# Carries of a pair of steps computed together on POOL in a selective state-space scan

## The chip, the cores and the metric

The kernel runs on one core of one Trainium2 chip. What counts is the device time of one execution in microseconds (us), as the median of several runs. The core's engines are TensorE (PE; its weight loads are listed as PEld), VectorE (DVE), ScalarE (ACT), GpSimd (POOL) and SyncE (SP), which issues the DMAs.

## What is computed

The reference is one block with a conditioned normalisation, a selective state-space layer that is run forwards and backwards over the sequence, and a gated MLP. Its input is 16 sequences of 256 positions with 256 channels, in float32. The part that sets the time is the recurrence, which is run over 512 inner channels with 64 states each:

```python
def step(hst, ins):
    dt_t, B_t, C_t, x_t = ins
    dA = jnp.exp(dt_t[:, :, None] * A)
    hst = hst * dA + (dt_t * x_t)[:, :, None] * B_t[:, None, :]
    y_t = jnp.einsum('bds,bs->bd', hst, C_t)
    return (hst, y_t)
...
_, ys = jax.lax.scan(step, h0, (tm(dt), tm(Bm), tm(Cm), tm(xs)))
y = jnp.swapaxes(ys, 0, 1) + xs * Dskip
return y * jax.nn.silu(z) @ out_w
```

## The kernel before

The main phase makes 16 passes (8 pairs of sequences, two directions). The 128 partitions hold 2 sequences by 64 states. A pass cuts its 256 positions into 8 chunks of 32 (`TC`), and the 512 channels into 16 groups of 32. One **step** j is one chunk and one group of channels, so a pass has 128 steps (`JP`), 16 to a chunk, and is taken two steps at a time: pair i is the steps 2i and 2i+1, 64 pairs a pass. The engines run the same list of steps side by side and are held together by semaphores:

- **PE**, step j: eight small matmuls write the step's inputs into the PSUM buffer `u[j % 2]` (L968), four write the exponents of step j+2 (L979), and eight add up a part of the last half chunk's output (L998). Before it, it waits for `ud` of the pair (POOL, L501), for `dd` of the pair after it (POOL, L492) and for the scan j-2, which frees `u`.
- **ACT**, step j: `put_carry(j)` (L755) copies the carry `hin` into the first column of each of the 32 channels of `u[j % 2]`. Then comes `decay(j + 2)`: twice an exponential of the first column (`e0`, named b_first in the rows, L736) and one of the other 31 columns (`dA`, L737). Then one piece of side work.
- **DVE**, step j: one scan over 1024 columns (L829), after `put_carry(j)`.
- **POOL**, pair i: `turn_dt(i + 2)` (L492), the carry of step 2i, side work, `turn_u(i + 1)` (L501), at i%8 = 2 `spread_c` (L514) and at i%8 = 6 `first_inputs` (L520), the carry of step 2i+1, side work. `turn_dt(i + 2)` waits for scan 2i-3.

A carry is needed from the second chunk of a pass on, that is for the steps 16 to 127 of each pass. It is `hin = e0 * hs_last + u0`: the first decay of the chunk times the last state of the same channels in the chunk before (`carry_in`, a product at L527 and a sum at L532, both over 32 columns), plus the first input. `e0`, `hm` and `hin` have four buffers (`NM`), by j % 4. In `hs` the two steps of a pair stand in neighbouring words (the last axis, `kp`).

The **side work** prepares the next pass: projections, SiLU and softplus of its inputs. It is written as generators (`unit`), of which each engine takes one piece a step, in the passes 0 to 14. On POOL pieces start with pair 2. One SiLU of the eight takes four steps: a clamp (L432) after the even carry of one pair, and the product (L438) after the odd carry of the next. The product waits for ACT's third sigmoid piece (L605). The four softplus parts follow, each with four pieces in four steps in a row (L444, L447, L451, L456), at the steps 42 to 45, 54 to 57, 68 to 71 and 80 to 83. Every second pass (0, 2 to 12) has four more pieces of normalisation in a row at the steps 102 to 105 (L423). POOL takes all of this in the order in which it is written.

After the main phase an output phase of some 450 us multiplies by the output weights and runs the MLP. The change doesn't touch it.

Of the kernel before, what the change touches and what calls it, by code (L numbers as in the profile page):

```python
# [6 lines left out]
ALU = mybir.AluOpType  # L7
# [19 lines left out]
TC = 32  # L27
# [5 lines left out]
STEPS = RT // 2 * SPN  # L33
# [25 lines left out]
def main_phase(nc, x, cond, w_mod, b_mod, w_in, w_xp, dt_bias, a_log, mod, scr):  # L59
# [4 lines left out]
    with ctx:  # L64
        def sb(name, shape, dt=fp32):
            return ctx.enter_context(nc.sbuf_tensor(name, shape, dt))
# [81 lines left out]
        hm_made = sem("b_hm_made")  # L148
# [6 lines left out]
        e0_done = sem("b_e0_done")  # L155
        hin_made = sem("b_hin_made")
        carried = sem("b_carried")
        scanned = sem("b_scanned")
# [37 lines left out]
        CSTEPS = JP - STEPS  # L196
# [18 lines left out]
        def scanned_to(p, j):  # L215
            return p * JP + (j + 1 + SCAN0)
# [4 lines left out]
        def carried_to(p, j):  # L221
            return p * CSTEPS + (j - STEPS + 1 + CARRY0)
# [10 lines left out]
        def place(j):  # L233
            c, k = divmod(j, STEPS)
            return c, k, k % 2, k // 2
# [6 lines left out]
        with nc.Block() as block:  # L242
# [162 lines left out]
            def _(pool):  # L405
# [99 lines left out]
                def spread_c(p, c):  # L505
                    n = c % 2
                    g = p * NCH + c
                    pool.wait_ge(c_loaded[n], loaded_to(p, c, C_DMAS))
                    if g >= 2:
                        pool.wait_ge(summed, QT * (2 * g - 2))  # L510
                    for b in range(CB):
                        first = b * QG
                        last = first + (QG - 1) * (QR + 1) + 1
                        nc.gpsimd.tensor_tensor(cw[:, n, :, first:last:QR + 1], cr[:, n, :, :],  # L514
                                                hmask[:, b:b + 1].unsqueeze(2).broadcast_to((P, QT, QG)), ALU.mult).then_inc(cw_made, 1)

                def first_inputs(p, c):
                    pool.wait_ge(f_loaded[c % 2], loaded_to(p, c, F_DMAS))
                    flat = u0[:, c % 2, :, :, :].rearrange("p k v d -> p (k v d)")
                    nc.gpsimd.tensor_tensor(flat, flat, b0[:, c % 2, :].broadcast_to((P, DI)), ALU.mult).then_inc(u0_made, 1)  # L520
                    pool.wait_ge(u0_made, p * (NCH - 1) + c)

                def carry_in(p, j):
                    c, k, kp, v = place(j)
                    pool.wait_ge(e0_done, p * (2 * CSTEPS) + 2 * (j - STEPS + 1))
                    pool.wait_ge(scanned, scanned_to(p, j - STEPS))
                    nc.gpsimd.tensor_tensor(hm[:, j % NM, :, :].rearrange("p h d -> p (h d)"),  # L527
                                            e0[:, j % NM, :, :].rearrange("p h d -> p (h d)"),
                                            hs[:, v, :, TC - 1, kp], ALU.mult).then_inc(hm_made, 1)
                    pool.wait_ge(hm_made, p * CSTEPS + (j - STEPS + 1))  # L530
                    pool.wait_ge(carried, carried_to(p, j - NM))
                    nc.gpsimd.tensor_tensor(hin[:, j % NM, :, :], hm[:, j % NM, :, :],  # L532
                                            u0[:, c % 2, 2 * kp:2 * kp + 2, v, :], ALU.add).then_inc(hin_made, 1)

                def ahead(p, i, turn, last):
                    if i < PAIRS:
                        turn(p, i)
                    elif not last:
                        turn(p + 1, i - PAIRS)

                def one_pass(p, last, side):
                    for i in range(PAIRS):
                        c, v = divmod(i, STEPS // 2)
                        ahead(p, i + 2, turn_dt, last)
                        if c:
                            carry_in(p, 2 * i)
                        if i >= 2:
                            next(side, None)
                        ahead(p, i + 1, turn_u, last)
                        if v == 2:  # L550
                            spread_c(p, c)
                        if v == STEPS // 2 - 2 and c + 1 < NCH:
                            first_inputs(p, c + 1)
                        if c:
                            carry_in(p, 2 * i + 1)
                        if i >= 2:
                            next(side, None)

# [3 lines left out]
                for p in range(PASSES):  # L562
                    one_pass(p, p == PASSES - 1, unit(p + 1) if p + 1 < PASSES else wait_steps(0))
# [894 lines left out]
```

## Time and profile before

| | |
|---|---|
| median of 3 runs | 5534.01 us (5531.95 to 5535.1) |
| time of the profiled execution | 5537.5 us |
| its span | 5535.8 us |
| mean granted TensorE clock of the span | 0.985 |
| main phase with carries, first to last `hin` | 155.1 to 5074.8 us |
| busy, PE / DVE / ACT / POOL | 5360.0 / 4737.6 / 3368.7 / 3918.4 us |

All three runs lie within 3.2 us of each other. A busy PE is not one at its peak: the ends of its matmuls are modelled, and they overlap. For the other engines a gap between two instructions is time in which the engine stood still, and the profile names what ended it. In the timelines an entry can stand for several instructions that follow each other without a gap (x2, x3). Every pass with side work looks like every other to within a few tenths of a microsecond, so pass 5 (it starts about 1674 us into the span) stands for them here. In pass 5 scan 16 starts at 1713.43 us, scan 42 at 1782.36 us and scan 80 at 1880.9 us. Pass 6 is 313.9 us later.

### The profile page before, as it was taken

To read this page: it belongs to the slowest core of one execution; us is meant where nothing else is said; L and a number is where in the kernel's file an instruction comes from. 1 tells how busy PE (TensorE), PEld (TensorE's weight loads), DVE (VectorE), ACT (ScalarE), POOL (GpSimd) and SP (SyncE) were. 2 spreads that over 40 slices of the span, in tenths; PEclk is the share of its full clock that TensorE was granted. 3 is DMA by queue.
4 is the path that set the end of the run, shared out by engine and by line. 5 is a ranking of instruction groups with operands and counts; after the bars stand their busy time and mean duration, and the time that the engine had idled before them with its cause. 6 is when DMAs were issued, how large, how long until landed. Compare 5 with 4: busy or idle time off the path is not lost. (4 is left out here: it accounts for less than half of the span.)

```text
span 5535.8 us, 127746 instructions
## 1 busy us (share of the span) xinstructions
PE 5360.0 (97%) x43632; PEld 2426.9 (44%) x43632; DVE 4737.6 (86%) x2419; ACT 3368.7 (61%) x11178; POOL 3918.4 (71%) x6629
## 2 busy tenths in 40 slices
PE   5999999999999999999999999999999999997898
PEld 3444444444444444444444444444444444443444
DVE  2898998989898998989898999989898998997433
ACT  4666666666666666666666666666666666564111
POOL 4777777787877777787877778787877778674221
PEclk8999999999999999999999999999999999998999
DMA  3111112111111112111111112111111111112552
GB/s 100 55 46 53 52 36 64 36 60 35 56 47 53 51 34 63 38 53 44 55 46 53 51 35 64 37 54 44 55 46 49 52 35 47 31 28 81 157 156 64
DMA packets 433131, 306.57 MB, mean 55 GB/s; under 512 B 215920, under 2 KB 336240, under 8 KB 432496
## 3 DMA queue, kind: packets, MB, share of 16 engines
q1 hardware_dynamic: 428272, 294.39, 17.8%
q8 instruction: 340, 5.57, 0.4%
q10 hardware_dynamic: 4224, 4.19, 0.2%
q14 instruction: 295, 2.42, 0.1%
HBM read 187.27 MB, written 111.15 MB: 54 GB/s over the span
## 5 line engine op out<-in xcount | busy, mean ns | idle before, releaser
L829 DVE TENSOR_TENSOR_SCAN b_hs<-b_dA,b_u 128x1024 f32<-128x1024 f32 x2048 | 4552.4, 2271 | 425.4 <-ACT b_u L755 351.8
L979 PE MATMUL b_ex<-b_dd,b_aw 32*128 32x512 f32 x8192 | 3081.6, 643 | 23.0 <-POOL b_dd L492 15.0
L737 ACT ACTIVATE b_dA<-b_ex 128x496 f32<-128x496 f32 x4096 | 2286.3, 588 | 254.2 <-PE b_ex L979 234.5
L968 PE MATMUL b_u<-b_ud,b_bw 32*128 32x256 f32 x16384 | 2344.8, 403 | 36.3 <-DVE b_hs L829 33.8
L968 PEld LDWEIGHTS b_u<-b_ud,b_bw 32*128 32x128 f32 x16384 | 1385.9, 184 | 1135.6 <-issue 697.8
L492 POOL TENSOR_TENSOR b_dd<-b_dr,b_mask 128x512 f32<-128x512 f32 x1024 | 1073.2, 1048 | 646.2 <-DVE b_hs L829 629.9
L998 PE MATMUL b_y<-b_hs,b_cw 128*32 128x256 f32 x16384 | 1261.3, 390 | 2.7 <-DVE b_hs L829 2.7
L755 ACT ACTIVATE b_u<-b_hin 128x32 f32<-128x32 f32 x1792 | 361.2, 202 | 1438.8 <-PE b_u L968 1040.8
L979 PEld LDWEIGHTS b_ex<-b_dd,b_aw 32*128 32x128 f32 x8192 | 1057.2, 183 | 161.3 <-ACT b_dA L737 104.0
L501 POOL TENSOR_TENSOR b_ud<-b_ur,b_mask 128x512 f32<-128x512 f32 x1024 | 1082.4, 1057 | 0.1
L998 PEld LDWEIGHTS b_y<-b_hs,b_cw 128*32 128x32 f32 x16384 | 348.6, 108 | 1196.7 <-issue 1150.2
L736 ACT ACTIVATE b_first<-b_ex 128x16 f32<-128x16 f32 x3584 | 629.7, 176 | 27.5 <-PE b_ex L979 22.9
L527 POOL TENSOR_TENSOR b_hm<-b_first,b_hs 128x32 f32<-128x32 f32 x1792 | 480.2, 268 | 120.6 <-ACT b_first L736 108.6
L532 POOL TENSOR_TENSOR b_hin<-b_hm,b_u 128x32 f32<-128x32 f32 x1792 | 450.5, 251 | 140.4
L1132 POOL TENSOR_TENSOR c_gs<-c_gs,c_sz 128x512 f32<-128x512 f32 x64 | 78.9, 1271 | 300.4 <-DVE c_gs L1338 300.4
L874 PE MATMUL b_job<-b_hT,b_win 128*128 128x512 f32 x488 | 276.0, 648 | 0.0
L887 PE MATMUL b_job<-b_xs,b_wxp 128*128 128x512 f32 x488 | 273.7, 644 | 0.0
L438 POOL TENSOR_TENSOR b_xs<-b_xs,b_cl 128x512 f32<-128x512 f32 x64 | 82.1, 1283 | 113.3 <-ACT b_cl L605 113.3
L432 POOL TENSOR_SCALAR b_cl<-b_xs 128x512 f32<-128x512 f32 x64 | 95.0, 1485 | 88.6 <-ACT b_xs L615 88.3
L748 ACT ACTIVATE b_ysb<-b_y 128x128 f32<-128x128 f32 x512 | 120.5, 308 | 8.9 <-PE b_y L998 8.9
L874 PEld LDWEIGHTS b_job<-b_hT,b_win 128*128 128x128 f32 x488 | 73.5, 189 | 118.6 <-issue 88.8
L444 POOL TENSOR_TENSOR b_nd<-b_wy,b_ey 128x512 f32<-128x512 f32 x64 | 82.0, 1281 | 56.5 <-ACT b_wy L638 56.5
(128 smaller groups left out, 2492.6 us busy)
## 6 DMA issues: line engine op xcount, KB each, us to landing
b_u<-scratch_ut SPq DMA_DIRECT2D x256, 128.0 KB, 2.9
scratch_y<-b_ysb SPq DMA_DIRECT2D x128, 256.0 KB, 2.3
scratch_xs<-b_xs SPq DMA_DIRECT2D x64, 256.0 KB, 2.2
scratch_sz<-b_sd SPq DMA_DIRECT2D x64, 256.0 KB, 3.3
scratch_dt<-b_sd SPq DMA_DIRECT2D x64, 256.0 KB, 2.0
scratch_ut<-b_uT SPq DMA_DIRECT2D x64, 256.0 KB, 2.3
b_ur<-scratch_ut SPq DMA_DIRECT2D x1024, 16.0 KB
b_dr<-scratch_dt SPq DMA_DIRECT2D x1024, 16.0 KB, 1.7
```

The lines of the kernel that those rows point to most:

```text
L492: nc.gpsimd.tensor_tensor(dd[:, i % NPR, :, :], dr[:, c % 2, v:v + 1, :].broadcast_to((P, TT, TC)), mask[:, :].unsqueeze(2).broadcast_to(( ...
L501: nc.gpsimd.tensor_tensor(ud[:, i % NPR, :, :, :], ur[:, c % 2, :, v * TT:(v + 1) * TT].unsqueeze(3).broadcast_to(shape), mask[:, :].unsqu ...
L527: nc.gpsimd.tensor_tensor(hm[:, j % NM, :, :].rearrange("p h d -> p (h d)"), e0[:, j % NM, :, :].rearrange("p h d -> p (h d)"), hs[:, v, : ...
L532: nc.gpsimd.tensor_tensor(hin[:, j % NM, :, :], hm[:, j % NM, :, :], u0[:, c % 2, 2 * kp:2 * kp + 2, v, :], ALU.add).then_inc(hin_made, 1)
L736: nc.scalar.activation(e0[:, j % NM, h, :], src[:, :, 0], ACT.Exp).then_inc(e0_done, 1)
L737: nc.scalar.activation(dA[:, j % NDA, h, :, 1:TC], src[:, :, 1:TC], ACT.Exp).then_inc(exp_done, 1)
L755: nc.scalar.activation(u[:, j % 2, :, 0:H:TC], hin[:, j % NM, :, :], ACT.Copy).then_inc(carried, 1)
L829: nc.vector.tensor_tensor_scan(hs[:, v, :, :, kp].rearrange("p d t -> p (d t)"), dA[:, j % NDA, :, :, :].rearrange("p h d t -> p (h d t)") ...
L874: ins = nc.tensor.matmul(job_bank(n)[:, :], win[:, k, i * P:(i + 1) * P], hT[:, q % DIRS, k, :], start=(k == 0), stop=(k == MB - 1))
L968: ins = nc.tensor.matmul(dst[:, :, tb, :], bw[row(r), c % 2, tb, :], ud[row(r), j // 2 % NPR, tb, :, :], start=(tb == 0), stop=(tb == NTB ...
L979: nc.tensor.matmul(e[bank_of(2 * j + h)][:, :], aw[row(r), p % DIRS, v, :, :].rearrange("p b s -> p (b s)"), dd[row(r), j // 2 % NPR, :, : ...
L998: ins = nc.tensor.matmul(y[q * QR:(q + 1) * QR, cols], cw[:, n, q, g * QR:(g + 1) * QR], hs[:, f * (SPN // 2):(f + 1) * (SPN // 2), :, q * ...
```

## The change

`carry_in` is called once a pair, for the even step 2i, and makes both carries: one product and one sum over 64 columns where there were two of each over 32. The call after `turn_u`, for step 2i+1, is gone. The waits are those that the odd step had: for its `e0` (ACT's `decay(2i+1)`), and for `put_carry(2i-3)`. The semaphores `hm_made` and `hin_made` go up by two.

```diff
                 def carry_in(p, j):
+
                     c, k, kp, v = place(j)
-                    pool.wait_ge(e0_done, p * (2 * CSTEPS) + 2 * (j - STEPS + 1))
-                    pool.wait_ge(scanned, scanned_to(p, j - STEPS))
-                    nc.gpsimd.tensor_tensor(hm[:, j % NM, :, :].rearrange("p h d -> p (h d)"),
-                                            e0[:, j % NM, :, :].rearrange("p h d -> p (h d)"),
-                                            hs[:, v, :, TC - 1, kp], ALU.mult).then_inc(hm_made, 1)
-                    pool.wait_ge(hm_made, p * CSTEPS + (j - STEPS + 1))
-                    pool.wait_ge(carried, carried_to(p, j - NM))
-                    nc.gpsimd.tensor_tensor(hin[:, j % NM, :, :], hm[:, j % NM, :, :],
-                                            u0[:, c % 2, 2 * kp:2 * kp + 2, v, :], ALU.add).then_inc(hin_made, 1)
+                    two = slice(j % NM, j % NM + 2)
+                    pool.wait_ge(e0_done, p * (2 * CSTEPS) + 2 * (j + 1 - STEPS + 1))
+                    pool.wait_ge(scanned, scanned_to(p, j + 1 - STEPS))
+                    nc.gpsimd.tensor_tensor(hm[:, two, :, :].rearrange("p j h d -> p j (h d)"),
+                                            e0[:, two, :, :].rearrange("p j h d -> p j (h d)"),
+                                            hs[:, v, :, TC - 1, :].rearrange("p d k -> p k d"), ALU.mult).then_inc(hm_made, 2)
+                    pool.wait_ge(hm_made, p * CSTEPS + (j + 1 - STEPS + 1))
+                    pool.wait_ge(carried, carried_to(p, j + 1 - NM))
+                    nc.gpsimd.tensor_tensor(hin[:, two, :, :].rearrange("p j h d -> p (j h) d"),
+                                            hm[:, two, :, :].rearrange("p j h d -> p (j h) d"),
+                                            u0[:, c % 2, :, v, :], ALU.add).then_inc(hin_made, 2)
...
                         if v == STEPS // 2 - 2 and c + 1 < NCH:
                             first_inputs(p, c + 1)
-                        if c:
-                            carry_in(p, 2 * i + 1)
                         if i >= 2:
                             next(side, None)
```

POOL's queue in the SiLU stretch of a pass, from one product of the side work to the next two steps on; b_first is `e0`, b_e0_done tells that ACT has made it. Before:

```order
L438 TENSOR_TENSOR b_xs<-b_xs,b_cl 128x512 [waits b_chain]
L492 TENSOR_TENSOR b_dd<-b_dr,b_mask 128x512 [waits b_scanned]
L527 TENSOR_TENSOR b_hm<-b_first,b_hs 128x32 [waits b_scanned,b_e0_done]
L532 TENSOR_TENSOR b_hin<-b_hm,b_u 128x32 [waits b_carried,b_hm_made]
L432 TENSOR_SCALAR b_cl<-b_sd 128x512 [waits b_silu_made,b_freed]
L501 TENSOR_TENSOR b_ud<-b_ur,b_mask 128x512 [waits b_scanned]
L527 TENSOR_TENSOR b_hm<-b_first,b_hs 128x32 [waits b_scanned,b_e0_done]
L532 TENSOR_TENSOR b_hin<-b_hm,b_u 128x32 [waits b_carried,b_hm_made]
L492 TENSOR_TENSOR b_dd<-b_dr,b_mask 128x512 [waits b_scanned]
```

The same place with the change:

```order
L438 TENSOR_TENSOR b_xs<-b_xs,b_cl 128x512 [waits b_chain]
L492 TENSOR_TENSOR b_dd<-b_dr,b_mask 128x512 [waits b_scanned]
L529 TENSOR_TENSOR b_hm<-b_first,b_hs 128x64 [waits b_scanned,b_e0_done]
L534 TENSOR_TENSOR b_hin<-b_hm,b_u 128x64 [waits b_carried,b_hm_made]
L432 TENSOR_SCALAR b_cl<-b_sd 128x512 [waits b_silu_made,b_freed]
L501 TENSOR_TENSOR b_ud<-b_ur,b_mask 128x512 [waits b_scanned]
L492 TENSOR_TENSOR b_dd<-b_dr,b_mask 128x512 [waits b_scanned]
```

The odd step's product and sum, which stood behind the clamp and `ud`, now stand ahead of both, in the same instructions as the even step's.

POOL's queue at the first softplus part (steps 42 to 46), before:

```order
L444 TENSOR_TENSOR b_nd<-b_wy,b_ey 128x512 [waits b_logged]
L501 TENSOR_TENSOR b_ud<-b_ur,b_mask 128x512 [waits b_scanned]
L527 TENSOR_TENSOR b_hm<-b_first,b_hs 128x32 [waits b_scanned,b_e0_done]
L532 TENSOR_TENSOR b_hin<-b_hm,b_u 128x32 [waits b_carried,b_hm_made]
L447 TENSOR_TENSOR b_nd<-b_ln,b_nd 128x512 [waits b_nd_made]
L492 TENSOR_TENSOR b_dd<-b_dr,b_mask 128x512 [waits b_scanned,b_d_loaded1]
L527 TENSOR_TENSOR b_hm<-b_first,b_hs 128x32 [waits b_scanned,b_e0_done]
L532 TENSOR_TENSOR b_hin<-b_hm,b_u 128x32 [waits b_carried,b_hm_made]
L451 TENSOR_TENSOR b_sd<-b_pre,b_nd 128x512 [waits b_sz_stored0,b_nd_made]
```

And with the change:

```order
L444 TENSOR_TENSOR b_nd<-b_wy,b_ey 128x512 [waits b_logged]
L501 TENSOR_TENSOR b_ud<-b_ur,b_mask 128x512 [waits b_scanned]
L447 TENSOR_TENSOR b_nd<-b_ln,b_nd 128x512 [waits b_nd_made]
L492 TENSOR_TENSOR b_dd<-b_dr,b_mask 128x512 [waits b_scanned,b_d_loaded1]
L529 TENSOR_TENSOR b_hm<-b_first,b_hs 128x64 [waits b_scanned,b_e0_done]
L534 TENSOR_TENSOR b_hin<-b_hm,b_u 128x64 [waits b_carried,b_hm_made]
L451 TENSOR_TENSOR b_sd<-b_pre,b_nd 128x512 [waits b_sz_stored0,b_nd_made]
```

Each softplus piece now waits behind a product that needs the `e0` of the pair's odd step; the small instructions between `ud` and the next piece are gone. On ACT, DVE, PE and SP the instructions and their order are unchanged.

## Rows read from the trace of the kernel before

**Rows 1.** Page, costliest groups: line, engine, out<-in, shape, count | busy us, mean ns | idle before, releaser

```profile
L829 DVE TENSOR_TENSOR_SCAN b_hs<-b_dA,b_u 128x1024 f32<-128x1024 f32 x2048 | 4552.4, 2271 | 425.4 <-ACT b_u L755 351.8
...
L501 POOL TENSOR_TENSOR b_ud<-b_ur,b_mask 128x512 f32<-128x512 f32 x1024 | 1082.4, 1057 | 0.1
...
L527 POOL TENSOR_TENSOR b_hm<-b_first,b_hs 128x32 f32<-128x32 f32 x1792 | 480.2, 268 | 120.6 <-ACT b_first L736 108.6
L532 POOL TENSOR_TENSOR b_hin<-b_hm,b_u 128x32 f32<-128x32 f32 x1792 | 450.5, 251 | 140.4
```

**Rows 2.** Waits, whole span: engine, line, who ended them, us in total, times, longest

```profile
ACT b_u L755 <- PE b_u L968: 1040.8, 1290, 2.1
...
ACT b_u L755 <- POOL b_hin L532: 397.3, 373, 2.6
DVE b_hs L829 <- ACT b_u L755: 351.8, 602, 2.3
```

**Rows 3.** DVE's timeline, pass 5, scans 10 to 15: start, length, [idle before <-releaser]

```profile
1698.51 6.64 DVE L829 TENSOR_TENSOR_SCAN b_hs<-b_dA,b_u 128x1024 f32<-128x1024 f32 x3 [0.20 <-PE b_u L968]
1705.82 2.29 DVE L829 TENSOR_TENSOR_SCAN b_hs<-b_dA,b_u 128x1024 f32<-128x1024 f32 x1 [0.67 <-PE b_u L968]
1708.53 4.46 DVE L829 TENSOR_TENSOR_SCAN b_hs<-b_dA,b_u 128x1024 f32<-128x1024 f32 x2 [0.42 <-PE b_u L968]
```

**Rows 4.** DVE's timeline, pass 5, the quiet scans 96 to 101

```profile
1914.80 13.15 DVE L829 TENSOR_TENSOR_SCAN b_hs<-b_dA,b_u 128x1024 f32<-128x1024 f32 x6
```

**Rows 5.** DVE's scans alone by stretch: from:to, length, busy (count), PEclk, DMA, GB/s

```profile
1712.00:1760.90 48.90, 41.61 (x19) 1.00 0.15 46
2025.80:2074.70 48.90, 41.70 (x19) 1.00 0.15 46
1782.30:1799.60 17.30, 13.61 (x6) 1.00 0.19 54
...
1880.90:1894.20 13.30, 13.12 (x7) 1.00 0.24 72
```

**Rows 6.** POOL's timeline, pass 5, SiLU stretch, around the carries of step 20

```profile
1733.34 0.27 POOL L527 TENSOR_TENSOR b_hm<-b_first,b_hs 128x32 f32<-128x32 f32 x1
1733.69 0.25 POOL L532 TENSOR_TENSOR b_hin<-b_hm,b_u 128x32 f32<-128x32 f32 x1
1733.90 1.48 POOL L432 TENSOR_SCALAR b_cl<-b_sd 128x512 f32<-128x512 f32 x1
...
1741.27 1.28 POOL L438 TENSOR_TENSOR b_sd<-b_sd,b_cl 128x512 f32<-128x512 f32 x1 [1.18 <-ACT b_cl L605]
```

**Rows 7.** ACT's timeline, same place: put_carry 21 and 22, sigmoid piece, put_carry 24

```profile
1737.00 0.20 ACT L755 ACTIVATE b_u<-b_hin 128x32 f32<-128x32 f32 x1 [1.19 <-POOL b_hin L532]
...
1739.36 0.20 ACT L755 ACTIVATE b_u<-b_hin 128x32 f32<-128x32 f32 x1 [0.52 <-PE b_u L968]
...
1740.55 0.65 ACT L605 ACTIVATE b_cl<-b_cl 128x512 f32<-128x512 f32 x1
...
1744.16 0.20 ACT L755 ACTIVATE b_u<-b_hin 128x32 f32<-128x32 f32 x1 [0.83 <-POOL b_hin L532]
```

**Rows 8.** POOL's timeline, pass 5, quiet stretch: the sum of step 98

```profile
1918.49 0.25 POOL L532 TENSOR_TENSOR b_hin<-b_hm,b_u 128x32 f32<-128x32 f32 x1
```

**Rows 9.** ACT's timeline, quiet stretch: last e0 of step 99, put_carry 98

```profile
1919.40 0.18 ACT L736 ACTIVATE b_first<-b_ex 128x16 f32<-128x16 f32 x1
...
1920.91 0.20 ACT L755 ACTIVATE b_u<-b_hin 128x32 f32<-128x32 f32 x1 [0.86 <-PE b_u L968]
```

**Rows 10.** POOL's timeline, first softplus part: its first piece, the product of step 46

```profile
1781.31 1.28 POOL L444 TENSOR_TENSOR b_nd<-b_wy,b_ey 128x512 f32<-128x512 f32 x1 [3.09 <-ACT b_wy L638]
...
1793.08 0.26 POOL L527 TENSOR_TENSOR b_hm<-b_first,b_hs 128x32 f32<-128x32 f32 x1
```

**Rows 11.** POOL's timeline, fourth softplus part: dd of two neighbouring pairs

```profile
1882.31 1.05 POOL L492 TENSOR_TENSOR b_dd<-b_dr,b_mask 128x512 f32<-128x512 f32 x1
...
1887.91 1.05 POOL L492 TENSOR_TENSOR b_dd<-b_dr,b_mask 128x512 f32<-128x512 f32 x1
```

## The prediction, made before the changed kernel was run

> **What bounds the kernel now.** I read first the page's groups, for the engine whose instructions fill the span, then the waits, for what interrupts it, then the timelines of one pass, for where. The scans of DVE are that engine: 2048 of them, 4552.4 us busy, and 425.4 us idle ahead of them, of which 351.8 behind ACT's put_carry [rows 1]. Six scans in a row take 13.15 us, so an undisturbed scan takes 2.19 us [rows 4], and the reader should take 4.38 us as the fastest possible pair. A lone one shows 2.29: each break costs its idle time and some 0.1 more. Put_carry is seldom late on its own account: 1290 times PE's matmuls into u released it, 373 times (397.3 us) POOL's sum hin [rows 2]. The first is the normal rhythm, since u becomes free only two scans back; the second is the part that this change can reach.
>
> Where it sits the timelines tell. Late in a pass POOL has hin for step 98 at 1918.74 and put_carry takes it at 1920.91, 2.2 us later [rows 8, 9]: nothing to gain there. In the SiLU stretch (steps 16 to 34) it is otherwise. The window 1712.00 to 1760.90 holds 18 scans and 1.0 us of the end of scan 15; 48.9 - 1.0 - 18 x 2.19 = 8.5 us are lost, and pass 6 has the same numbers [rows 3, 5]. In the first softplus part six scans take 17.3 us where 13.15 would do, 4.1 lost [rows 5]. PE has pauses of its own for the projections: before step 16, where no carry exists, PE is named as the releaser of 0.67 and 0.42 us at two neighbouring steps, 1.25 with the 0.1 of each break, and of 0.20, some 0.3, where it has less output work [rows 3].
>
> **What the change removes and adds.** Product and sum show 268 and 251 ns [rows 1], but what POOL's queue pays is the distance between starts: 0.35 from product to sum, 0.21 from sum to the next instruction [rows 6], 0.56 us a carry, 1.12 a pair. For 64 columns no row exists. Between 32 and 512 columns the price grows by (1057 - 251)/480 = 1.7 ns a column [rows 1], or, with two full operands, (1280 - 251)/480 = 2.1 [rows 1, 6]. So 32 more columns cost 0.05 to 0.07 us an instruction; I take 0.05, as both forms repeat little data and are short, and 0.66 us for the pair. The outer bound is that they cost what a second instruction costs (0.27 and 0.25 more). POOL saves 1.12 - 0.66 = 0.46 us a pair, and 896 pairs have carries: 412 us, nearly all of it on an engine that is waited for only at places.
>
> The Trainium skill, "Perfetto Trace Analysis", section "GPSIMD Engine Instruction", holds a GpSimd instruction's shown span unreliable and would have it timed by the spacing of starts. By spans alone the saving would be 2 x (0.27 + 0.25) - 0.62 = 0.42 us a pair and the sum below would move by a tenth; the trace agrees that they differ (0.27 shown, 0.35 spaced) [rows 6].
>
> **What the change delays.** Even carries now wait for the odd step's e0. In the quiet stretch the last e0 of step 99 ends at 1919.58; 0.08 to start, 0.40 to the sum, 0.30 for it: hin at 1920.36, and put_carry 98 is ready at 1920.91 [rows 9]. The slack of 2.2 us shrinks to 0.5, but stays, and it stays in every quiet pair, since each of its links (put_carry 97, decay 99, carry, put_carry 98) is fixed. On the path: nothing. What it costs is POOL's lead: side work, ud and dd are queued behind the waiting product. ud of the next pair is there 0.66 + 1.06 = 1.8 us after that e0, or 3.1 with a side piece ahead of it; PE wants it when scan 2i ends, some 3.8 us after e0. Nobody waits.
>
> **Steps 16 to 34.** The cycle there: ACT's third sigmoid piece ends at 1741.20, after put_carry 22 at 1739.36; POOL's product has stood waiting 1.18 us for it, then come dd and the carry of step 24, and put_carry 24 follows at 1744.16 [rows 6, 7]. That is 4.80 us where 4.38 would do; with 64 columns 4.9, so 0.5 to 0.55 late instead of 0.4. Then the odd carry: put_carry 21 at 1737.00 waited 1.19 us for hin [rows 7], because clamp and ud stand ahead of it. With the change it is ready with the even one, and this wait of 0.7 to 1.9 us in each four steps goes. What is late next: again the 0.55 at each fourth step, or PE's own pauses (0.3 in one cycle, 1.25 in the next [rows 3]). The POOL wait comes at the step where PE would pause one step later, so I let the larger count, not the sum. Five cycles: 0.6 + 1.25 + 0.55 + 1.4 + 0.55 = 4.35 us; the 1.4 is the cycle with first_inputs, one 1.0 us instruction more before the next even carry. Saved: 8.5 - 4.35 = 4.1 us a pass.
>
> **First softplus part.** From its first piece at 1781.31 to the product of step 46 at 1793.08 POOL works without a pause [rows 10]. Two odd carries leave that stretch (1.12), two even ones widen (0.10) and the sum of step 46 widens too (0.1): step 46 comes 0.9 us earlier. Saved 0.9.
>
> **The other bursts.** Fourth part: dd to dd is 5.60 us a pair [rows 11], 1.22 over 4.38, for two pairs 2.4, which the lead of 2.2 now covers almost (seven entries fill 13.12 of 13.30 us [rows 5]). With the change 5.14 a pair, 0.76 over, 1.5 for two, of which a lead of 0.5 covers a third: 1.0 late where it was 0.2. Lost 0.8. The second and third parts have the same overrun, but PE pauses by itself around them; I put 0 and 0.2. The normalisation pieces at the steps 102 to 105 (seven passes) are like the fourth part: 7 x 0.8 = 6 us.
>
> **Sum.** 4.1 + 0.9 - 0.8 - 0.2 = 4.0 us in each of 15 passes with side work = 60, less 6: 54 us. From the profiled execution's 5537.5 that is 5483.5; it stood 3.5 over the median, so **5480 us**.
>
> **Rivals.** (a) *POOL's lateness goes whole*: the third sigmoid piece comes early enough, and only PE's pauses are left. Steps 16 to 34 then lose 0.3 + 1.25 + 0.3 + 1.25 + 0.3 = 3.4, the softplus part saves twice the 0.9 and the bursts are hidden: 5.1 + 1.8 = 6.9 x 15 = 103 us, 5431 us. For it: POOL has 0.46 us more room in each pair. Against: the cycle over ACT doesn't get shorter.
> (b) *The lead is worth more than the work*: the pauses of PE and the new waits behind e0 add up instead of overlapping. Then the bursts cost 1.0 + 1.2 + 0.8 each pass and the cycle 2 us more: 4.1 - 2 + 0.9 - 3.0 = 0, with the 6 us of normalisation 5534 + 6 = 5540; halfway 5515. For it: each burst overruns and the lead falls from 2.2 to 0.5. Against: PE's pauses lie near them.
> (c) *Slower*: the 64-column forms, with a third dimension and the states 64 words apart, cost as two of 32. The point where it decides is 0.5 us on product plus sum together, the slack of every quiet pair. At the bound (0.52 more) POOL saves nothing, every even put_carry is at its limit or 0.05 late (some 40 pairs a pass: 2 us), and each burst is late by its whole overrun: 2.4 x 4 less what PE's pauses hide (3) and what is lost now, + 5; the odd waits of steps 16 to 34 still go, - 3. Some 4 to 5 us a pass: 5600 us. Against: a column costs 2 ns between 32 and 512.
> (d) *It doesn't do what it says*: the waits named after POOL are PE's in truth. Then nothing but (b)'s losses, 5545 to 5560. Against: after a wait for hin of 1.19 us [rows 7] DVE's loss in the window is too large for PE's pauses, 8.5 us against 3.4.
>
> **Chances.** Forecast 0.62, (a) 0.14, (b) 0.15, (c) 0.05, (d) 0.04. The range reaches from (a) to halfway into (b): 5430 to 5520. A measurement of this kernel can tell 0.2%, 11 us. Faster 0.82, the same 0.09, slower 0.09.
>
> **What would show it.** Product and sum at 0.30 to 0.34 us each, 896 times; the waits of put_carry for hin down from 397 us to near 150; the waits of the product for e0 up from 108.6 us to some 1000 us in the quiet pairs, and harmless; SiLU window 1712.0 to 1760.9 shorter by 4 us; a break of about 1 us at step 84. Wrong if a quiet pair takes more than 4.38 us (c), if the SiLU window still loses 8 us (d), or if breaks of over 1 us stand at the steps 56 to 58 and 72 (b).

## The result: the changed kernel is slower

The changed kernel takes 5557.02 us (median of 5 runs, 5553.83 to 5563.28) against 5534.01 us before, a ratio of 1.0046 with a 95% interval of 1.0034 to 1.0057. Forecast were 5480 us and a range of 5430 to 5520. The profiled execution after took 5557.02 us, its span is 5555.3 us and its mean granted clock 0.985, as before. The time is lost in the main phase: its last scan starts at 5078.2 us before and at 5097.7 after.

The page of the changed kernel, costliest groups, beside [rows 1] (its lines from `carry_in` on have higher numbers: L830 is the scan, L756 put_carry, L738 and L737 the exponentials, L969 and L980 PE's inputs and exponents, L999 its output groups):

```profile
L830 DVE TENSOR_TENSOR_SCAN b_hs<-b_dA,b_u 128x1024 f32<-128x1024 f32 x2048 | 4554.8, 2272 | 441.7 <-ACT b_u L756 369.4 <-PE b_u L969 63.8 <-issue 1.9
...
L529 POOL TENSOR_TENSOR b_hm<-b_first,b_hs 128x64 f32<-128x64 f32 x896 | 316.7, 353 | 938.4 <-ACT b_u L756 895.5 <-issue 41.4
L534 POOL TENSOR_TENSOR b_hin<-b_hm,b_u 128x64 f32<-128x64 f32 x896 | 287.7, 321 | 122.2 <-issue 4.6 <-DVE b_hs L830 0.4
```

The waits, beside [rows 2]:

```profile
ACT b_u L756 <- PE b_u L969: 1218.7, 1463, 2.3
...
POOL b_hm L529 <- ACT b_u L756: 895.5, 572, 3.8
...
DVE b_hs L830 <- ACT b_u L756: 369.4, 642, 1.5
...
ACT b_u L756 <- POOL b_hin L534: 229.1, 201, 2.1
```

Put_carry waited for hin 229.1 us where it was 397.3, and for PE 1218.7 where it was 1040.8. One wait took the other's place, and what DVE waits for put_carry rose by 18 us. The product's 938 us of idle time are the wait for the odd step's e0; the profile names another instruction of ACT for it, but in the quiet pair shown further down (a pair with no side work on POOL) the product starts at 1924.43, 0.13 us after the end of that e0 on ACT.

DVE's scans alone in the windows that answer [rows 5], moved to where the same steps lie (steps 16 to 34, 42 to 48, 80 to 86 of pass 5):

```profile
1723.00:1771.80 48.80, 41.27 (x19) 1.00 0.15 45
1793.10:1809.70 16.60, 13.61 (x6) 1.00 0.20 57
1888.80:1903.00 14.20, 12.98 (x7) 1.00 0.25 71
```

The differences between the starts of scans, from DVE's timelines of both kernels, don't depend on where a window is cut (pass 5, us; the last row pass 6):

| from scan, to scan | before | after | after less before |
|---|---|---|---|
| 14 to 16 | 4.90 | 5.12 | +0.22 |
| 16 to 34, SiLU stretch | 47.54 | 47.57 | +0.03 |
| 34 to 42 | 21.38 | 21.07 | -0.31 |
| 42 to 48, first softplus part | 17.33 | 16.67 | -0.66 |
| 54 to 62, second part | 20.83 | 21.45 | +0.62 |
| 62 to 80, third part | 43.33 | 43.35 | +0.02 |
| 80 to 86, fourth part | 13.39 | 14.50 | +1.11 |
| 100 to 108, normalisation | 18.27 | 19.16 | +0.89 |

The first seven lines stand for each of the 15 passes with side work, the last for seven passes: (0.22 + 0.03 - 0.31 - 0.66 + 0.62 + 0.02 + 1.11) x 15 = 15.5, and 0.89 x 7 = 6.2, 21.7 us in all. The last scan starts 19.5 us later. Summed over all passes as they are, the same eight stretches give 26.2 us. To that come 1.0 us ahead of the first scan and 0.1 in small places, and the steps 48 to 54, which the table leaves out, take 7.8 us less: 19.5.

The steps 48 to 54 are where the passes are not alike. Before, they take 14.04 us in most passes and 15.2 to 17.1 in five (2, 5, 6, 7, 11), and in just these five the granted clock fell to the 1.2 GHz level there: a short spell costs 1.1 to 1.3 us, one of twice the length 2.8 to 3.0. After, only pass 6 has such a spell, but five passes have one at the steps 56 and 57, which is why the steps 54 to 62 lose 12.7 us over all passes and not 15 x 0.62 = 9.3.

### The profile page after: what moved, and what is told of

Same layout as the page of the kernel before. It is cut to its first block and busy times, and to the rows that moved or that the text cites. A ratio compares the mean times of both kernels' runs of the same rounds, so it can differ in the third digit from the quotient of the medians.

```text
span 5555.3 us, 124258 instructions
## 1 busy us (share of the span) xinstructions
PE 5376.9 (97%) x43632; PEld 2423.1 (44%) x43632; DVE 4740.1 (85%) x2419; ACT 3374.5 (61%) x11178; POOL 3629.3 (65%) x4837
## 5 line engine op out<-in xcount | busy, mean ns | idle before, releaser
L830 DVE TENSOR_TENSOR_SCAN b_hs<-b_dA,b_u 128x1024 f32<-128x1024 f32 x2048 | 4554.8, 2272 | 441.7 <-ACT b_u L756 369.4
L980 PE MATMUL b_ex<-b_dd,b_aw 32*128 32x512 f32 x8192 | 3063.1, 643 | 28.3 <-POOL b_dd L492 15.1
L738 ACT ACTIVATE b_dA<-b_ex 128x496 f32<-128x496 f32 x4096 | 2290.9, 589 | 254.1 <-PE b_ex L980 233.0
L969 PE MATMUL b_u<-b_ud,b_bw 32*128 32x256 f32 x16384 | 2354.0, 404 | 34.6 <-DVE b_hs L830 32.9
L969 PEld LDWEIGHTS b_u<-b_ud,b_bw 32*128 32x128 f32 x16384 | 1378.0, 184 | 1130.4 <-issue 737.3
L999 PE MATMUL b_y<-b_hs,b_cw 128*32 128x256 f32 x16384 | 1261.0, 390 | 2.7 <-DVE b_hs L830 2.7
L756 ACT ACTIVATE b_u<-b_hin 128x32 f32<-128x32 f32 x1792 | 361.4, 202 | 1448.4 <-PE b_u L969 1218.7
L980 PEld LDWEIGHTS b_ex<-b_dd,b_aw 32*128 32x128 f32 x8192 | 1041.6, 183 | 208.5 <-ACT b_dA L738 154.3
L529 POOL TENSOR_TENSOR b_hm<-b_first,b_hs 128x64 f32<-128x64 f32 x896 | 316.7, 353 | 938.4 <-ACT b_u L756 895.5
L999 PEld LDWEIGHTS b_y<-b_hs,b_cw 128*32 128x32 f32 x16384 | 348.8, 108 | 1177.6 <-issue 1130.7
L737 ACT ACTIVATE b_first<-b_ex 128x16 f32<-128x16 f32 x3584 | 631.2, 176 | 27.4 <-PE b_ex L980 22.8
L534 POOL TENSOR_TENSOR b_hin<-b_hm,b_u 128x64 f32<-128x64 f32 x896 | 287.7, 321 | 122.2 <-issue 4.6
L438 POOL TENSOR_TENSOR b_sd<-b_sd,b_cl 128x512 f32<-128x512 f32 x64 | 82.1, 1283 | 82.4 <-ACT b_cl L606 82.4
```

Source lines behind the costliest of these rows:

```text
L529: nc.gpsimd.tensor_tensor(hm[:, two, :, :].rearrange("p j h d -> p j (h d)"), e0[:, two, :, :].rearrange("p j h d -> p j (h d)"), hs[:, v, ...
L534: nc.gpsimd.tensor_tensor(hin[:, two, :, :].rearrange("p j h d -> p (j h) d"), hm[:, two, :, :].rearrange("p j h d -> p (j h) d"), u0[:, c ...
L737: nc.scalar.activation(e0[:, j % NM, h, :], src[:, :, 0], ACT.Exp).then_inc(e0_done, 1)
L738: nc.scalar.activation(dA[:, j % NDA, h, :, 1:TC], src[:, :, 1:TC], ACT.Exp).then_inc(exp_done, 1)
L756: nc.scalar.activation(u[:, j % 2, :, 0:H:TC], hin[:, j % NM, :, :], ACT.Copy).then_inc(carried, 1)
L830: nc.vector.tensor_tensor_scan(hs[:, v, :, :, kp].rearrange("p d t -> p (d t)"), dA[:, j % NDA, :, :, :].rearrange("p h d t -> p (h d t)") ...
```

## Why the SiLU stretch kept its time

This is the change's own place, where 4.1 us a pass were forecast and nothing came: 18 scans need 18 x 2.19 = 39.4 us, and 8.1 us are lost in both kernels. DVE's timeline of the changed kernel, scans 16 to 20 of pass 5:

```profile
1724.47 4.46 DVE L830 TENSOR_TENSOR_SCAN b_hs<-b_dA,b_u 128x1024 f32<-128x1024 f32 x2 [0.66 <-ACT b_u L756]
1729.86 4.46 DVE L830 TENSOR_TENSOR_SCAN b_hs<-b_dA,b_u 128x1024 f32<-128x1024 f32 x2 [0.93 <-ACT b_u L756]
1734.87 2.29 DVE L830 TENSOR_TENSOR_SCAN b_hs<-b_dA,b_u 128x1024 f32<-128x1024 f32 x1 [0.55 <-ACT b_u L756]
```

And before, the same scans:

```profile
1713.43 2.29 DVE L829 TENSOR_TENSOR_SCAN b_hs<-b_dA,b_u 128x1024 f32<-128x1024 f32 x1 [0.44 <-ACT b_u L755]
1716.46 6.82 DVE L829 TENSOR_TENSOR_SCAN b_hs<-b_dA,b_u 128x1024 f32<-128x1024 f32 x3 [0.74 <-ACT b_u L755]
1723.61 2.29 DVE L829 TENSOR_TENSOR_SCAN b_hs<-b_dA,b_u 128x1024 f32<-128x1024 f32 x1 [0.33 <-ACT b_u L755]
```

The odd scan 17 now follows at once, and scan 18 waits 0.93 us instead: the same time one step later. From scan 16 to scan 18 there are 5.4 us in both. ACT's timelines show the same for put_carry 16, 18 and 20. Before:

```profile
1713.10 0.20 ACT L755 ACTIVATE b_u<-b_hin 128x32 f32<-128x32 f32 x1 [0.68 <-POOL b_hin L532]
...
1718.49 0.20 ACT L755 ACTIVATE b_u<-b_hin 128x32 f32<-128x32 f32 x1 [0.52 <-PE b_u L968]
...
1723.28 0.20 ACT L755 ACTIVATE b_u<-b_hin 128x32 f32<-128x32 f32 x1 [0.83 <-POOL b_hin L532]
```

After:

```profile
1724.13 0.20 ACT L756 ACTIVATE b_u<-b_hin 128x32 f32<-128x32 f32 x1 [0.90 <-POOL b_hin L534]
...
1729.53 0.20 ACT L756 ACTIVATE b_u<-b_hin 128x32 f32<-128x32 f32 x1 [1.40 <-PE b_u L969]
...
1734.54 0.20 ACT L756 ACTIVATE b_u<-b_hin 128x32 f32<-128x32 f32 x1 [1.04 <-POOL b_hin L534]
```

16 to 18: 5.39 us before and 5.40 after. 18 to 20: 4.79 and 5.01 us. The first part doesn't contain the odd carry. It runs from put_carry 16 over `decay(18)` on ACT, which frees the PSUM banks for the exponents of PE's step 17, and then through PE's queue. Weight loads of the changed kernel:

```profile
1725.51 0.29 PEld L980 LDWEIGHTS b_ex<-b_dd,b_aw 32*128 32x128 f32 x2 [0.21 <-ACT b_dA L738]
1726.56 0.16 PEld L999 LDWEIGHTS b_y<-b_hs,b_cw 128*32 128x32 f32 x8 [0.76 <-issue]
1727.13 0.30 PEld L875 LDWEIGHTS b_job<-b_hT,b_win 128*128 128x128 f32 x2 [0.41 <-issue]
1728.18 0.19 PEld L969 LDWEIGHTS b_u<-b_ud,b_bw 32*128 32x128 f32 x2 [0.76 <-POOL b_dd L492]
```

Exponents behind dA, the output group, the projection, and only then the inputs of step 18, 4.05 us after put_carry 16; before they also stand 4.05 us behind it (1717.15 and 1713.10). The releaser POOL named in the last row had long been done. So the late odd carry at scan 17, 0.74 us of idle DVE, lay beside a longer way and cost nothing. From scan to scan the whole stretch is, in pairs of steps from 16 to 34: before 5.39, 4.79, 5.89, 4.79, 5.39, 4.80, 6.35, 4.74, 5.39 us, after 5.39, 5.01, 5.68, 5.01, 5.39, 5.02, 5.67, 5.01, 5.39. The odd waits of 0.74 and 1.14 us (scans 17, 21, 25, 33) are hidden. The one of 1.86 at scan 29, behind `first_inputs`, is not:

```profile
1748.64 6.64 DVE L829 TENSOR_TENSOR_SCAN b_hs<-b_dA,b_u 128x1024 f32<-128x1024 f32 x3 [1.86 <-ACT b_u L755]
```

There the change did save 0.68 us, and it saved 0.21 at 20 to 22; the four pairs that became 0.22 to 0.27 us longer took it back. These longer pairs are the second part, from put_carry 18 over the third sigmoid piece and POOL to put_carry 20. It does contain the pair's product and sum, and these take longer over 64 columns. POOL's timeline in a quiet pair of the changed kernel:

```profile
1924.43 0.35 POOL L529 TENSOR_TENSOR b_hm<-b_first,b_hs 128x64 f32<-128x64 f32 x1 [1.51 <-ACT b_u L756]
1924.91 0.32 POOL L534 TENSOR_TENSOR b_hin<-b_hm,b_u 128x64 f32<-128x64 f32 x1
1925.19 1.06 POOL L501 TENSOR_TENSOR b_ud<-b_ur,b_mask 128x512 f32<-128x512 f32 x1
```

From start to start 0.48 and 0.28 us, where [rows 6] has 0.35 and 0.21: 0.20 us a pair, not 0.10. POOL saves 1.12 - 0.76 = 0.36 us a pair.

That gives **theory A**: (1) in steps 16 to 34 the even put_carry goes round two ways, 5.4 us over decay and PE and 4.8 us over the sigmoid piece and POOL; the odd carry is in neither; (2) the wait for the odd e0 takes POOL's lead (the time by which a carry is ready before it is needed), and bursts of side work (two pieces in one pair) then make carries late. **Theory B**: what costs is the width of the new instructions.

## The experiments

Each was run in turns with the kernel before; the ratios are to it, with their 95% interval.

### e1: the wait alone

```diff
-                    pool.wait_ge(e0_done, p * (2 * CSTEPS) + 2 * (j - STEPS + 1))
+                    pool.wait_ge(e0_done, p * (2 * CSTEPS) + 2 * (j + 1 - j % 2 - STEPS + 1))
```

> The kernel before with one wait changed: the even carry waits for the odd step's e0 as in the changed kernel, but its product and sum stay at 32 columns and the odd carry stays at its own place. Theory A (the wait takes POOL's lead away, and bursts of side work then show): nothing in steps 16 to 34, where the odd e0 is there in time; late carries behind the four-piece bursts at steps 58, 72, 84 and 106, 3 to 5 us a pass, so 5580 to 5610 us. Theory B (the width of the 64-column instructions is what costs): the kernel before's time, 5534 to 5540 us.

Measured: 5600.54 us, 1.0122 (1.0107 to 1.0138). From scan 16 to scan 34 of pass 5 it has 47.54 us, as before. Behind the fourth softplus part, scans 80 to 86, 14.91 us. DVE's timeline there:

```profile
1914.09 2.29 DVE L829 TENSOR_TENSOR_SCAN b_hs<-b_dA,b_u 128x1024 f32<-128x1024 f32 x1 [0.50 <-ACT b_u L755]
1916.89 2.29 DVE L829 TENSOR_TENSOR_SCAN b_hs<-b_dA,b_u 128x1024 f32<-128x1024 f32 x1 [0.52 <-ACT b_u L755]
1919.69 6.64 DVE L829 TENSOR_TENSOR_SCAN b_hs<-b_dA,b_u 128x1024 f32<-128x1024 f32 x3 [0.51 <-ACT b_u L755]
```

Three breaks at the steps 82, 83 and 84 where there was one of 0.18. The loss sits behind the bursts: over all passes the steps 54 to 62 lose 22 us, the third part 4, the steps 80 to 86 22 and the steps 100 to 108 15. The steps 14 to 48, with the first softplus part in them, keep their time to 0.1 us, and the steps 48 to 54 take 8 us less, with one spell of low clock instead of five. Theory A's second half is shown, and B falls as the only cause: without one wide instruction the wait costs 68 us, three times the loss of the changed kernel.

### e2: both carries at the even place, as two of 32 columns each

```diff
                         if c:
                             carry_in(p, 2 * i)
+                            carry_in(p, 2 * i + 1)
...
-                        if c:
-                            carry_in(p, 2 * i + 1)
```

(in the kernel before)

> The changed kernel's places, but product and sum of the even step and then of the odd step as four instructions over 32 columns, the even pair waiting only for its own e0. Theory A: in steps 16 to 34 the even put_carry is as late as before the change (4.80 us after the one two steps back), not 0.2 later, and the odd wait is gone without the cycle of four steps becoming shorter; behind the bursts breaks as in the changed kernel or longer, since POOL saves nothing: 5560 to 5590 us. Theory B: place alone is harmless, so the time of the prediction's gain, 5480 to 5530 us.

Measured: 5546.56 us, 1.0021 (1.0012 to 1.0030), 13 us under A's span and well over B's. DVE's timeline, scans 16 to 20:

```profile
1719.29 4.46 DVE L828 TENSOR_TENSOR_SCAN b_hs<-b_dA,b_u 128x1024 f32<-128x1024 f32 x2 [0.44 <-ACT b_u L754]
1724.68 4.46 DVE L828 TENSOR_TENSOR_SCAN b_hs<-b_dA,b_u 128x1024 f32<-128x1024 f32 x2 [0.93 <-ACT b_u L754]
1729.49 2.29 DVE L828 TENSOR_TENSOR_SCAN b_hs<-b_dA,b_u 128x1024 f32<-128x1024 f32 x1 [0.34 <-ACT b_u L754]
```

The idle times of the even scans are those of before (0.44 and 0.34, before 0.44 and 0.33), the odd wait is gone, and the 0.93 stands at scan 18 all the same. That shows the first half of A for the scans 17, 21, 25 and 33 with no instruction changed in size: the pairs there keep their times to 0.02 us. A is not right for scan 29. From scan 28 to scan 30 e2 takes 5.88 us where the kernel before takes 6.35, and the steps 16 to 34 fall from 47.54 to 47.17: of the odd carry's wait of 1.86 us some 0.4 a pass, 6 us in all, were on the path.

A had the bursts too dear: they cost e2 0.97 us in the fourth part (14.36 against 13.39) where I had thought of more than the changed kernel's 1.11. The even sum doesn't wait for the odd e0 here and keeps its lead; that this is the reason was not tested by itself. Against the changed kernel four narrow instructions do better than two wide ones by 10 us, but that is not the width alone, since the wait differs too. In the steps 14 to 34 it can be told apart, because e1 shows that the wait costs nothing there: 4.90 + 47.17 us in e2 against 5.12 + 47.57, 0.6 us a pass or 9 us for the width, which is on the way of the even carry. Behind the bursts e2 is better by about as much again, from both causes, and in the traces its spells of low clock at the steps 48 to 54 hide that.

### e3: the pair's carry ahead of dd

```diff
-                        ahead(p, i + 2, turn_dt, last)
                         if c:
                             carry_in(p, 2 * i)
+                        ahead(p, i + 2, turn_dt, last)
```

(in the changed kernel)

> The changed kernel with the pair's carry moved ahead of turn_dt(i + 2), so that dd no longer stands between the SiLU product and the even carry. Theory A (the cycle of four steps in the SiLU stretch is the even put_carry after the third sigmoid piece, 5.0 us, plus 5.4 us over decay and PE): the first falls to the floor of 4.4, 0.6 us a cycle, 3 us a pass, so 5505 to 5520 us, with the breaks behind the bursts unchanged. Rival (PE's own pauses fill what POOL gives): 5545 to 5560 us.

Measured: 5524.34 us, 0.9985 (0.9976 to 0.9994): 33 us under the changed kernel, 4 us short of A's span. The steps 16 to 34 fall to 46.46 us. What A had not seen is in the timeline of scans 17 to 22:

```profile
1715.43 2.29 DVE L830 TENSOR_TENSOR_SCAN b_hs<-b_dA,b_u 128x1024 f32<-128x1024 f32 x1 [0.15 <-ACT b_u L756]
1718.38 6.64 DVE L830 TENSOR_TENSOR_SCAN b_hs<-b_dA,b_u 128x1024 f32<-128x1024 f32 x3 [0.67 <-ACT b_u L756]
1726.36 2.29 DVE L830 TENSOR_TENSOR_SCAN b_hs<-b_dA,b_u 128x1024 f32<-128x1024 f32 x1 [1.33 <-ACT b_u L756]
```

The even scans 18 and 20 stand in one row, and every second cycle (scan 21) pauses 1.33 us: there PE has two output groups, and no carry is late. Only each second cycle gains: from scan 16 to scan 20 9.77 us against 10.40 in the changed kernel, from scan 20 to scan 24 10.88 against 10.68.

### e5 and e6: the side pieces two steps apart, in the changed kernel and in the one before

```diff
-                        yield from softplus(q, j)
-                        yield from wait_steps((8, 10, 8, 12)[j])
+                        for _ in softplus(q, j):
+                            yield
+                            yield
+                        yield from wait_steps((4, 4, 4, 10)[j])
...
-                        yield from wait_steps(6)
+                        yield from wait_steps(2)
                         for t in range(TB):
                             normalise(c, t)
                             yield
+                            yield
```

> The changed kernel with the pieces of each softplus part and of the normalisation on POOL put two steps apart instead of one, starts at steps 42, 54, 66 and 78 (normalisation 98). Theory A: no pair has two pieces, the breaks of 0.8 to 1 us at steps 58, 82 to 84 and 104 to 106 go, 1.8 us a pass and 6 us in all: 5520 to 5530 us. Theory B: unchanged, 5550 to 5560 us.

> The kernel before (carries apart, 32 columns) with the softplus and normalisation pieces two steps apart, as in e5. Theory A: it loses little behind bursts as it is (0.2 us at step 84, and the late carries at steps 44 to 46), so it gains only 0.3 to 0.8 us a pass: 5520 to 5530 us, within some 0.2% of e5; the bursts are what sets the changed kernel back against the kernel before. Theory B: nothing moves, 5530 to 5536 us.

Measured: e5 5515.86 us, 0.9966 (0.9954 to 0.9978); e6 5515.61 us, 0.9969 (0.9957 to 0.9980). Both gained more than expected, e5 41 us on the changed kernel and e6 18 us on the one before. The breaks of the fourth part at the scans 82 and 84 are gone in e5. The first row holds the scans 79 to 84, and what is left is 0.22 us at scan 85:

```profile
1870.44 13.15 DVE L833 TENSOR_TENSOR_SCAN b_hs<-b_dA,b_u 128x1024 f32<-128x1024 f32 x6
1883.81 4.47 DVE L833 TENSOR_TENSOR_SCAN b_hs<-b_dA,b_u 128x1024 f32<-128x1024 f32 x2 [0.22 <-ACT b_u L759]
```

Without bursts the two kernels are level: the 23 us between them are the bursts. The traces also tell where the gains are. On the changed kernel, over all passes: 4.6 us at the steps 42 to 48, 13.7 at 54 to 62, 16.5 at 80 to 86, 6.9 at 100 to 108, together the 41. On the kernel before: 14.0 us at the steps 42 to 48 (17.33 to 16.39 in each pass, where I had put too little), and 6.7 at the steps 48 to 54, where only two passes still have a spell of low clock.

### e15: the wait alone, without bursts

The edits of e1 and e6 together.

> e1 (carries apart, the even one waiting for the odd step's e0) with the pieces two steps apart. Theory A: the wait costs only where two pieces fall in one pair; a pair with one piece keeps POOL busy for 4.35 of 4.38 us, so the 68 us that the wait costs in e1 go: 5513 to 5522 us, level with e6. Rival (the wait costs something in every pair): at least 5535 us.

Measured: 5518.32 us, 0.9974 (0.9963 to 0.9985). The wait that cost 68 us in e1 costs 3 us here (e6 to e15), within the spread. What costs is the wait together with two pieces in one pair.

### e7 and e14: both edits, with the carries merged and with the carries apart

e7 is the changed kernel with the edits of e3 and e5. e14 is the kernel before with the same two.

> The changed kernel with both edits, the pair's carry ahead of dd (e3) and the pieces apart (e5). Theory A: the two act at different steps (16 to 34, and behind the bursts), so their gains of 33 and 41 us add: 5480 to 5490 us. Rival (POOL as a whole has one overload, and either edit relieves it): 5505 to 5515 us.

> The kernel before with the even carry ahead of dd and the pieces apart: e7 without the merging. In steps 16 to 34 the even carry is on time, the odd one now has dd, the clamp and ud ahead of it. Theory A: the odd wait grows to about 1.2 us, more than PE's part hides, so 5495 to 5510 us, 5 to 20 us over e7: here merging pays at last. Rival (the odd carry stays hidden): as e7 or some us below it, 5485 to 5492 us, since 32 columns are ready sooner.

Measured: e7 5490.92 us, 0.9923 (0.9909 to 0.9936); e14 5514.43 us, 0.9962 (0.9948 to 0.9975). The gains of e3 and e5 add up to 66 of 74 us. Put_carry waits for hin 11.6 us in the whole of e7:

```profile
ACT b_u L759 <- POOL b_hin L537: 11.6, 16, 0.9
```

In e14 the odd carry has dd, clamp and ud ahead of it, and DVE shows it, scan 17:

```profile
1710.31 6.64 DVE L832 TENSOR_TENSOR_SCAN b_hs<-b_dA,b_u 128x1024 f32<-128x1024 f32 x3 [1.20 <-ACT b_u L758]
```

That is more than PE's way hides: from scan 16 to scan 18 e14 takes 5.69 us, e7 5.39. Here merging is worth 24 us, 4 more than the upper end of what was expected.

### e10 and e11: PE's output groups moved, before and after

The table gives, for the step's number k%8, which output groups PE computes in it.

```diff
-        GROUP_AT = {1: (0,), 2: (1,), 3: (2,), 4: (3, 4), 5: (5,), 6: (6,), 7: (7,)}
+        GROUP_AT = {2: (0, 1), 3: (2, 3), 6: (4, 5), 7: (6, 7)}
```

> The kernel before, where PE adds up the output groups at the steps k%8 = 2, 3, 6 and 7 in twos, that is at the steps without a projection piece, instead of one at each of the steps 1 to 7 and two at step 4. Theory A (in the SiLU stretch the way from put_carry 4k to put_carry 4k+2 is decay, PE's exponents, output group, projection, inputs, 5.4 us or more, and hid the late odd carry): the pauses at steps 1 to 15 fall by about 1 us a pass, and in steps 16 to 34 the odd carry's wait becomes the limit, a light cycle of four steps 1.3 us over the floor instead of 1.46: 5495 to 5515 us. Rival (the pauses are the clock's or the DMAs'): 5530 to 5540 us.

> The changed kernel with the output groups moved as in e10. Theory A: with PE's part shorter the early odd carry now pays: the pause at steps 18 and 26 falls from 1.0 to 0.5 us or less, a light cycle to 1.1, and the changed kernel gains more by this edit than the kernel before does (e10): 5500 to 5520 us, against 5557. Rival (the odd carry never mattered): the same gain for both.

Measured: e10 5745.33 us, 1.0375 (1.0361 to 1.0389); e11 5678.73 us, 1.0254 (1.0238 to 1.0270). Both are far outside of what was expected, and most of it is the granted clock. The cores' view of e10 and of e11:

```profile
core 0: 5747.7 us, clock 0.951
```

```profile
core 0: 5682.8 us, clock 0.958
```

In the main phase the clock stands at its lower level for 437 us in e10 and 352 in e11, against 38 before and 31 after. An estimate from the stretches without such a spell (medians over the passes, the stretches of the table and those between): e10 would be 2.3 us a pass slower than the kernel before, some 34 us of its 211, and e11 1.2 us a pass faster than the changed kernel. The rest goes with the clock. So even without it e10 would have missed its 5495 to 5515 us.

In the SiLU stretch the clock of pass 5 is 1.00 all the same, and there the runs answer the question. Scans 16 to 34: e10 46.73 us, e11 44.67. DVE's timeline of e10, scans 19 to 22, and of e11, scans 20 to 23:

```profile
1781.50 4.47 DVE L829 TENSOR_TENSOR_SCAN b_hs<-b_dA,b_u 128x1024 f32<-128x1024 f32 x2 [0.30 <-ACT b_u L755]
1787.11 4.46 DVE L829 TENSOR_TENSOR_SCAN b_hs<-b_dA,b_u 128x1024 f32<-128x1024 f32 x2 [1.14 <-ACT b_u L755]
```

```profile
1770.13 4.46 DVE L830 TENSOR_TENSOR_SCAN b_hs<-b_dA,b_u 128x1024 f32<-128x1024 f32 x2 [0.55 <-ACT b_u L756]
1774.95 4.46 DVE L830 TENSOR_TENSOR_SCAN b_hs<-b_dA,b_u 128x1024 f32<-128x1024 f32 x2 [0.35 <-ACT b_u L756]
```

With PE's way shorter the odd carry's 1.14 us at scan 21 are on the path in e10 (from scan 20 to scan 22 it takes 5.61 us, e11 4.82), and merging saves 2.1 us in these 18 steps, half of the forecast. The mechanism of the prediction exists; in the kernel as it is, PE's way was the longer one.

### e12 and e13: fewer groups moved, on top of e7

e12, one group moved from k%8 = 4 to 3:

```diff
-        GROUP_AT = {1: (0,), 2: (1,), 3: (2,), 4: (3, 4), 5: (5,), 6: (6,), 7: (7,)}
+        GROUP_AT = {1: (0,), 2: (1,), 3: (2, 3), 4: (4,), 5: (5,), 6: (6,), 7: (7,)}
```

e13, none left at 4:

```diff
-        GROUP_AT = {1: (0,), 2: (1,), 3: (2,), 4: (3, 4), 5: (5,), 6: (6,), 7: (7,)}
+        GROUP_AT = {1: (0,), 2: (1,), 3: (2, 3), 5: (4,), 6: (5,), 7: (6, 7)}
```

> e7 with one of the two output groups that PE adds at k%8 = 4 put to k%8 = 3, nothing else. Theory A: PE's part after the even put_carry sets the cycles, so those with two groups (pauses 1.42 and 0.53 at steps 21 and 22; 0.75 and 0.53 at 5 and 6) fall by some 0.5 us each, four times a pass: 5455 to 5470 us, if the granted clock stays at 0.987. If it falls as in e10, slower than e7.

> e7 with no output group at k%8 = 4: 0, 1, 2 and 3, 4, 5, 6 and 7 at the steps 1, 2, 3, 5, 6 and 7. Theory A: pauses of the cycles at 21 and 5 fall by another 0.4 us: 5440 to 5460 us with the clock at 0.987. Rival: a second step without output work lets the granted clock fall as in e10, and the time rises over e7's.

Measured: e12 **5457.31 us**, 0.9857 (0.9842 to 0.9872), 75 us under the kernel before and the fastest version here; e13 5531.89 us, 0.9996 (0.9987 to 1.0005). The granted clocks are 0.986 and 0.987, so e13's miss is not the clock. Scans 20 to 22 of e12 and 16 to 21 of e13:

```profile
1698.05 2.29 DVE L833 TENSOR_TENSOR_SCAN b_hs<-b_dA,b_u 128x1024 f32<-128x1024 f32 x1 [0.31 <-ACT b_u L759]
1700.82 2.29 DVE L833 TENSOR_TENSOR_SCAN b_hs<-b_dA,b_u 128x1024 f32<-128x1024 f32 x1 [0.49 <-ACT b_u L759]
1703.53 4.46 DVE L833 TENSOR_TENSOR_SCAN b_hs<-b_dA,b_u 128x1024 f32<-128x1024 f32 x2 [0.42 <-ACT b_u L759]
```

```profile
1712.19 4.46 DVE L833 TENSOR_TENSOR_SCAN b_hs<-b_dA,b_u 128x1024 f32<-128x1024 f32 x2 [0.42 <-ACT b_u L759]
1717.59 4.46 DVE L833 TENSOR_TENSOR_SCAN b_hs<-b_dA,b_u 128x1024 f32<-128x1024 f32 x2 [0.93 <-ACT b_u L759]
1722.36 4.49 DVE L833 TENSOR_TENSOR_SCAN b_hs<-b_dA,b_u 128x1024 f32<-128x1024 f32 x2 [0.31 <-ACT b_u L759]
```

In e12 scan 21 waits 0.49 us where it waited 1.33 in e7, and scan 20 got 0.31: a second group at step 3 delays step 4 by itself. In e13 each double group, now at 3 and 7, costs 0.3 to 0.4 at the step behind it, also in the quiet stretch, and scan 18 keeps its 0.93, since the group at step 17 is on PE's way as before. I had taken the groups at k%8 = 4 for the whole of PE's excess.

## Why the prediction was wrong, point by point

- **Steps 16 to 34, the step that failed.** Forecast: the odd wait goes, the 0.55 us at the fourth step and PE's pauses of 0.3 and 1.25 overlap ("I let the larger count, not the sum"), 4.1 us a pass saved, 61 us in 15 passes. Measured: 0.03 us. The odd waits went, but the prediction counted them as if they were on the path: four of the five lay beside PE's way, and the fifth (scan 29) gave 0.4 us (e2). PE's pauses there are not those of the steps 1 to 15: with carries they begin at put_carry, since PE's exponents wait for a `decay` that stands behind put_carry on ACT. In e3, where no even carry of these steps is late, they can be read alone: 1.33 + 0.42 and the 0.1 of each break, 1.95 us, in one cycle, and 0.39 + 0.43 + 0.2, 1.0 us, in the next, where 1.25 and 0.3 were put. And a late even carry doesn't overlap with them, it is what they start from: 5.40 + 5.01 us is a sum. The trace of the kernel before shows it: put_carry 18 follows put_carry 16 after 5.39 us with PE as its releaser, and [rows 7] names PE ahead of put_carry 22 too. This step is 62 of the 77 us between forecast and measurement.
- **Width of the instructions.** Forecast 0.10 us a pair, measured 0.20; on the even way five times a pass (at step 16 and in the four longer pairs); against e2, 0.6 us a pass in all. By the spans alone (0.353 and 0.321 against 0.268 and 0.251) it would be 0.16; the distance of starts shows 0.20.
- **Quiet pairs.** Slack forecast 0.5, measured 0.38 (sum ends 1925.23, put_carry 1925.61). No pair became longer: right.
- **First softplus part.** Forecast -0.9, measured -0.66 and -0.31 in the steps ahead of it, -0.97 together: right.
- **Bursts.** Fourth part forecast +0.8, measured +1.11: dd to dd takes 5.25 us there (1891.52 and 1896.77 on POOL) where 5.14 was put, and the slack is 0.38 where 0.5 was put. Second part forecast 0 under cover of PE's pauses, measured +0.62: scan 58 waits 0.80 us, which replaces the 0.88 that scan 59 waited before, but scan 60 then waits 0.83 instead of 0.42. Third part forecast +0.2, measured 0. Normalisation forecast +0.8, measured +0.89.
- **The rivals.** (b), that pauses and waits add up and the lost lead outweighs the saved work, is the mechanism that the runs show; it was given 0.15. Its 5540 us were 17 short although it put the bursts too high (3.0 us a pass, measured 1.75), because it still left 2.1 us a pass of the stretch's gain, 31 us, where nothing was left. Its own signs, breaks of over 1 us at the steps 56 to 58 and 72, did not appear: 0.80 at scan 58 and none at 72. (d) was named for a stretch that still loses 8 us, with 5545 to 5560 us, and both came true. It can't be put aside as wholly wrong: its reason (the waits named after POOL are PE's) doesn't hold, since the odd waits went with the change, but its consequence does, since PE's way stood beside them. That the measured time lies in its range owes nothing to its reason. (a) falls, as the even carries are later than before, and (c) too: no quiet pair passed 4.38 us, and the width costs 0.20 us a pair, not 0.52.
- **The other signs it named.** Product and sum at 0.30 to 0.34 us: 0.353 and 0.321. Waits for hin near 150 us: 229. Waits of the product for e0 some 1000 us and harmless: 938, and not harmless where a burst follows (e1). A break of about 1 us at step 84: 0.80, and 0.42 at 82.

The gain of e5 and e6 at the steps 42 to 48 is read from the traces, but no run moved the pieces of that part alone. Open is also what makes the clock fall at the steps 48 to 57 in some passes and not in others.

## What to carry to other kernels

A wait that ends last at its own step may still be off the path of the loop (here the odd carry's 0.74 and 1.14 us, but not its 1.86): measure the loop from one event to the same event a period later (here put_carry 16 to 18 to 20), and count a saving only if the removed work is on that way. Before merging two small instructions into one, see what the earlier half then waits for, and what lead the engine had: an average load under 1 doesn't help where side work comes in bursts. Here two other edits, an order on one queue and the spacing of side work, made the merging pay, 24 us, where alone it cost 23.

## What the runs showed of the hardware

- A product on POOL over 64 columns took 353 ns against 268 over 32, and 0.48 us from start to start against 0.35: 4 ns a column, twice the 1.7 to 2.1 between 32 and 512 columns of other operands. Its second operand steps over 64 words. The sum behind it grew from 0.21 to 0.28 us, 2.2 ns a column.
- The same matmuls in another order went with about 3 points less of granted clock: 0.951 in e10 and 0.958 in e11 against 0.985. In both, the steps with k%8 = 0, 1, 4 and 5 have no output group, where before only k%8 = 0 has none, and in the main phase the lower level of 1.2 GHz came back 68 and 56 times against 8 before and 8 after. With one group moved (e12) or four (e13: two steps of eight without a group) the clock stayed at 0.986 and 0.987.
- At the steps 48 to 54 a short spell at 1.2 GHz cost the scans 1.1 to 1.4 us and one of twice its length 2.8 to 3.0 us (kernel before, e2, e3, e7, e14).
